# A Perceiver layer: both groups of a pair sorted in joint VectorE instructions, with a new ScalarE order

## What is computed

```python
k = k @ Wk.T                                    # 256 features, 16 heads of 16
x = abs(where(k >= 0, k, 0.01 * k)) + EPS
nrm = x.mean(-1)
k = softmax(log(x) * focusing_factor, -1) * nrm # "focus", over all 256 features
# in each head only the 11 largest of the 16 features are kept
kv = einsum('bnc,bnd->bcd', k_kept, v)          # sums over all rows of a batch
```

## Time and profile of the kernel before

| | us |
|---|---|
| median of 3 runs | 470.62 (470.41 to 471.29) |
| the profiled execution | 470.4 |
| its span, first to last instruction | 468.7 |
| around the span | 1.7 |
| VectorE busy | 447.6 (96%) |
| TensorE matmuls busy | 386.4 (82%) |
| ScalarE busy | 360.4 (77%) |

### The profile page before, as it was taken

How to read it: one execution, slowest core, us unless ns; L and a number is a source line. 1 busy time by engine, 2 the same in 40 slices (tenths; PEclk the granted TensorE clock), 3 DMA queues, 4 the chain that set the end, 5 groups by cost and what they waited for, 6 DMA issues and landing times.

```text
span 468.7 us, 6040 instructions
## 1 busy us (share of the span) xinstructions
PE 386.4 (82%) x1931; PEld 306.3 (65%) x1934; DVE 447.6 (96%) x685; ACT 360.4 (77%) x950; POOL 6.2 (1%) x22
## 2 busy tenths in 40 slices
PE   7986758989989998998997997991999899648567
PEld 6775547877877876886785885891987445314334
DVE  6999999999999999999999999999998889899995
ACT  2679997997997997997888978885438678666765
POOL 2001000000000000000000000000000000000000
PEclk9999879999999999999999999997799999956968
DMA  6990000320220220230140040022020000000001
GB/s 224 348 324 2 1 1 1 97 82 2 90 90 2 91 90 1 68 113 1 46 134 1 28 132 22 2 92 88 1 90 1 0 1 1 0 0 1 22 23 46
DMA packets 27071, 27.66 MB, mean 59 GB/s; under 512 B 1184, under 2 KB 26784, under 8 KB 27040
## 3 DMA queue, kind: packets, MB, share of 16 engines
q1 hardware_dynamic: 26736, 27.27, 18.2%
q0 software_dynamic: 160, 0.01, 0.0%
q10 hardware_dynamic: 144, 0.00, 0.0%
HBM read 26.22 MB, written 1.05 MB: 58 GB/s over the span
## 4 chain that ended last, share of the span: by engine, by line
DVE 86%; PE 6%; ACT 4%; issue 2%; DMA 1%; SPq 0%; DVEq 0%
DVE mask L1405 8%; DVE focus_words L1325 8%; DVE focus_words L1305 8%; DVE sorted L1361 4%; DVE merge L1374 4%; DVE sorted L1362 4%; DVE level L1331 4%; DVE level L1332 4%; DVE sorted L1234 3%; DVE amax L1203 2%; DVE sorted L1367 2%; DVE sorted L1366 2%; DVE keymax L1364 2%; DVE merge L1372 2%; DVE rank L1385 2%
## 5 line engine op out<-in xcount | busy, mean ns | idle before, releaser
L817 PE MATMUL bank<-WkT,rows_T 128*128 128x256 f32 x512 | 123.8, 388 | 29.4 <-ACT rows_T L434 29.4
L817 PEld LDWEIGHTS bank<-WkT,rows_T 128*128 128x128 f32 x512 | 94.3, 192 | 46.2 <-ACT rows_T L434 35.2
L909 PE MATMUL bank<-ctx_words,focus_words 128*128 128x257 f32 x512 | 115.3, 383 | 2.8 <-ACT focus_words L533 2.8
L909 PEld LDWEIGHTS bank<-ctx_words,focus_words 128*128 128x128 f32 x512 | 99.5, 197 | 15.1 <-ACT focus_words L533 4.4
L521 ACT ACTIVATE focus_words<-focus_words,shift,ff 128x256 f32<-128x256 f32 x136 | 79.8, 590 | 0.6
L487 ACT ACTIVATE focus_words<-bank 128x256 f32<-128x256 f32 x136 | 50.1, 382 | 25.7 <-PE bank L817 25.7
L533 ACT ACTIVATE focus_words<-focus_words,row_scale 128x256 f32<-128x256 f32 x136 | 56.2, 515 | 11.3 <-DVE row_scale L1318 11.3
L434 ACT ACTIVATE rows_T<-bank 128x512 f32<-128x512 f32 x78 | 44.3, 595 | 17.1 <-PE bank L790 16.9
L790 PE MATMUL bank<-ident,ctx_words 128*128 128x128 f32 x256 | 37.5, 275 | 3.8 <-DMA ctx_words<-in_ctx_dram 3.5
L1405 DVE TENSOR_TENSOR mask<-focus_words,fifth 128x2048 bf16<-128x2048 f32 x17 | 39.0, 2292 | 0.5
L790 PEld LDWEIGHTS bank<-ident,ctx_words 128*128 128x128 f32 x256 | 31.0, 142 | 11.7 <-DMA ctx_words<-in_ctx_dram 6.2
(11 more groups left out here) (207 smaller groups left out, 589.3 us busy)
## 6 DMA issues: line engine op xcount, KB each, us to landing
ctx_words<-in_ctx_dram SPq DMA_DIRECT2D x32, 512.0 KB, 3.9
ctx_words<-in_L_ffn_gate_w_dram SPq DMA_DIRECT2D x2, 1024.0 KB, 6.7
ctx_words<-in_L_ffn_up_w_dram SPq DMA_DIRECT2D x2, 1024.0 KB, 8.2
xs<-in_x_dram SPq DMA_DIRECT2D x4, 256.0 KB, 5.0
ctx_words<-in_L_ffn_down_w_dram SPq DMA_DIRECT2D x2, 512.0 KB, 10.7
ctx_words<-in_L_ffn_down_w_dram SPq DMA_DIRECT2D x1, 1024.0 KB, 4.8
out_dram<-xs SPq DMA_DIRECT2D x3, 256.0 KB, 2.1
gateT<-in_L_attn_W_qkv_dram SPq DMA_DIRECT2D x1, 512.0 KB, 7.0
```

The costliest lines, as they stand in the source:

```text
L817: ins = pe.matmul(proj_bank[m][:, t * D:(t + 1) * D], rows_T[:, m % 2, 2 * t + k, :], WT[:, k, :], start=(k == 0), stop=(k == KT - 1))
L909: ins = pe.matmul(sum_bank[k][:, 0:GW], heads_half(expo[slot][:, t, :], k), ctx_ring[:, s, t, :], start=(s == 0 and t == 0), stop=(s == PE ...
```

## The change

For the rounds a = 3 to 13:

- **DVE.** `level1`, `sorted4`, `rowmax` and the like get 16 tiles instead of 8, and the keys of both groups lie side by side. `sort_fours_of_both` replaces two `compare_pairs` and two `sort_fours`: 12 instructions over sixteen tiles (one comparison is cut in two) instead of 20 over eight. The row maxima of both groups come out together. `make_keys(d)` moves to the end of the round (in round 1 too; the last round has one `make_keys` less). `apply_mask(a)` comes directly behind `make_mask(a)`, with a `settle()` between, and `inverse_sums` behind it, with a `settle()` ahead of `row_scales`. `rank` and `low8` now lie in the memory of `level1`, which adds a `settle()` in the last round.
- **ACT.** The two small instructions on the row maxima run once for both groups. The order of the round is new (below); `logarithms` of the coming a moves to the end of the round before, and `scale_rows(a)` moves behind all four lifts of d and the weight quads.
- Buffers swap places (`key[0]` and `expo[0]`, and with them two buffers of the later part); PE's and SP's programs are as before.

The core of the diff:

```diff
@@ ACT pair(a, last)
-                logarithms(a, at(a))
+                if a == 1:
+                    logarithms(a, at(a))
...
+                else:
+                    rows_to_sbuf(c, 0)
+                    rows_to_sbuf(c, 1)
+                    logarithms(b, at(b))
+                    exponentials(a, at(a), FORE_TILES)
+                    rows_to_sbuf(c, 2)
+                    exponentials(a, at(a), HIND_TILES)
+                    rows_to_sbuf(c, 3)
+                    lift(c, 0, at(c))
+                    rows_to_sbuf(d, 0)
+                    lift(c, 1, at(c))
+                    rows_to_sbuf(d, 1)
+                    exponentials(b, at(b), FORE_TILES)
+                    lift(c, 2, at(c))
+                    rows_to_sbuf(d, 2)
+                    lift(c, 3, at(c))
+                    exponentials(b, at(b), HIND_TILES)
+                    rows_to_sbuf(d, 3)
+                    if at(a) == 0:
+                        save_sums((a - 1) // PER_BATCH)
+                    for m in range(PAIRS):
+                        lift(d, m, at(d))
+                if not last:
                     if d in REST_BEHIND:
                         q = QK_QUADS + 2 * REST_BEHIND.index(d)
                         weight_quad(q)
                         weight_quad(q + 1)
-                    lift(d, 2, at(d))
-                    lift(d, 3, at(d))
+                    scale_rows(a, at(a))
+                    logarithms(c, at(c))
                 scale_rows(b, at(b))
@@ DVE sort_fours_of_both(a), new
+                settle()
+                dve.wait_ge(keyed, a + 2)
+                step(tt(level1[:, :, 1:4:2, :], keys_of_both[:, :, 0:4:2, :], keys_of_both[:, :, 1:4:2, :], ALU.max))
+                for at in (of_pair(a), of_pair(a + 1)):
+                    step(tt(level1[:, at, 0:4:2, :], keys_of_both[:, at, 0:4:2, :], keys_of_both[:, at, 1:4:2, :],
+                            ALU.min))
+                    if at.start == 0:
+                        settle(but=1)
+                        step(tt(sorted4[:, :, 3, :], level1[:, :, 1, :], level1[:, :, 3, :], ALU.max))
                 settle(but=1)
                 step(dve.tensor_reduce(keymax[:, :], sorted4[:, :, 3, :], AX.X, ALU.max))
                 settle(but=1)
+                step(tt(sorted4[:, :, 2, :], level1[:, :, 0, :], level1[:, :, 2, :], ALU.max))
                 settle(but=1)
+                row_maxima(both, 2)
+                step(tt(sorted4[:, :, 0:5:4, :], level1[:, :, 0:2, :], level1[:, :, 2:4, :], ALU.min))
+                settle()
+                inner_twos(both)
+                join_fours(both)
@@ DVE pair(a, last), rounds 3 to 13
+                    sort_fours_of_both(a)
                     find_fifths(slice(0, 2 * T))
                 make_mask(a)
...
+                        dve.wait_ge(expo_ready, a + 1)
+                        settle()
+                        apply_mask(a, at(a))
+                        inverse_sums(b, BOTH_SLOTS)
                     settle()
                     row_scales(b, BOTH_SLOTS)
                 make_mask(b)
...
                     make_keys(c, at(c))
                     settle()
                     apply_mask(b, at(b))
+                    make_keys(d, at(d))
```

More of the change, by code:

```diff
@@ L508, in exponentials @@
                 slot = (s + 1) % 2
+                first = of_pair(n).start
                 if tiles[0] == 0:
[L511 to L514, removed]
+                    if searched_alone(n) or n % 2:
+                        of, count = (of_pair(n), 1) if searched_alone(n) else (slice(0, 2 * T), 2)
+                        act.wait_ge(rowmax_ready, n + count)
+                        act.activation(lnmax[:, of], rowmax[:, of], ACT.Ln, bias=EPS).then_inc(lnmax_done, count)
+                        act.wait_ge(lnmax_done, n + count)
+                        act.activation(shift[:, of], lnmax[:, of], ACT.Identity, scale=ff_neg[:, 0:1])\
+                            .then_inc(shift_done, count)
                     act.wait_ge(shift_done, n + 1)
@@ L553, in pair @@
                     tail_rows_to_sbuf("sums1", (proj_in_psum, PAIRS * (CGROUPS + 1)))
[L554 to L561, removed]
+                    exponentials(a, at(a), ALL_TILES)
+                    logarithms(b, at(b))
+                    if at(a) == 0:
+                        save_sums((a - 1) // PER_BATCH)
                     tail_rows_to_sbuf("sums2", (kv_in_psum, 1))
@@ L564, in pair @@
                     exponentials(b, at(b), ALL_TILES)
-                else:
+                elif a == 1:
+                    rows_to_sbuf(c, 0)
+                    rows_to_sbuf(c, 1)
+                    exponentials(a, at(a), ALL_TILES)
+                    logarithms(b, at(b))
+                    save_sums(0)
                     exponentials(b, at(b), FORE_TILES)
@@ L1348, in half_keys_and_pairs, with join_fours @@
                 step(tt(level1[:, tiles, 1:4:2, :], k4[:, :, 0:4:2, :], k4[:, :, 1:4:2, :], ALU.max))
-            def of_pair(n):
-                return slice(0, T) if n % 2 or n == 0 else slice(T, 2 * T)
             low, high = merge[:, :, 0:4, :], merge[:, :, 4:6, :]
             first_of, second_of = slice(0, HEADS), slice(HEADS, 2 * HEADS)
+            def join_fours(at):
+                settle(but=1)
+                step(tt(high[:, at], sorted4[:, at, 0:2, 0:32], sorted4[:, at, 0:2, 32:64], ALU.max))
+                settle(but=1)
+                step(tt(low[:, at], sorted4[:, at, 0:4, 0:32], sorted4[:, at, 0:4, 32:64], ALU.min))
@@ L1357, in sort_fours, with inner_twos, row_maxima @@
+            def inner_twos(at):
+                step(tt(sorted4[:, at, 1, :], sorted4[:, at, 4, :], sorted4[:, at, 2, :], ALU.min))
+                step(tt(sorted4[:, at, 2, :], sorted4[:, at, 4, :], sorted4[:, at, 2, :], ALU.max))
+            def row_maxima(at, groups):
+                dve.tensor_scalar(rowmax[:, at].bitcast(I32), keymax[:, at].bitcast(I32), -HD, key_flip[:, 0:1],
+                                  ALU.bitwise_and, ALU.bitwise_xor).then_inc(rowmax_ready, groups)
             def sort_fours(n):
-                slot, at = n % 2, of_pair(n)
+                at = of_pair(n)
@@ L1469, in pair @@
                 else:
-                    inverse_sums(b, BOTH_SLOTS)
-                    settle(but=1)
-                    apply_mask(a, at(a))
+                    if a == 1:
+                        inverse_sums(b, BOTH_SLOTS)
+                        settle(but=1)
+                        apply_mask(a, at(a))
+                    else:
+                        dve.wait_ge(expo_ready, a + 1)
+                        settle()
+                        apply_mask(a, at(a))
+                        inverse_sums(b, BOTH_SLOTS)
                     settle()
```

93 lines of the change are left out of this document (56 added, 37 removed).

## The result

| | us |
|---|---|
| before, median of 4 runs | 470.96 (470.41 to 471.98) |
| after, median of 4 runs | 500.62 (499.54 to 502.5) |
| ratio | 1.063 (95%: 1.0608 to 1.0651) |
| the profiled execution of after | 502.5, its span 500.7 |

What follows compares the result with a forecast made beforehand. The PE, ACT and load loop, 38.1 us against DVE's 36.3, was taken to bound the changed kernel: 470.4 plus 16.7 for the loop plus 12.6 for six clock falls gives 499.7, say 500; range 484 to 504.

Steps and rivals of the forecast that it cites:

- The six falls: TensorE's clock falls ahead of each sum of groups 1 to 11, at 2.1 us each, 12.6 together.
- DVE's list: DVE's instructions in rounds 3 to 13: 0.5 us saved a round, 36.3 instead of 36.8.
- The 0.11 for a new hole: Each new settle on DVE, as at apply_mask(a) behind make_mask(a), costs 0.11 us; two cost 0.22 a round.
- The loop: From one sum_group(a) to the next through load, PE and ACT: 38.1 us, plus save_sums and weight quads in some rounds.
- Both links: sum_group(a)'s start to quad 2 of c ready, 17.9 us; then ACT to scale_rows(a)'s end, 18.9 plus 1.3 of waits.
- the terms 18.9, 1.3, 0.6 and 1.1: From quad 2 of c to scale_rows(a)'s end: ACT's work 18.9 us, waits for PE 1.3, save_sums 0.6, weight quads 1.1.
- its wait for PE ahead of quad 2 of c: ACT, in rounds 3 to 13, would wait some 4 us for PE to have quad 2 of c ready.
- DVE's waits for the exponentials: DVE idle 2 to 5 us a round ahead of inverse_sums, until ACT's exponentials of b are done.
- The clock: PE idle 4.2 to 5.0 us ahead of sum_group(a) lowers TensorE's clock; each fall costs 1.7 to 2.5 us.
- The rival with the clock up: The loop is the bound but PE's gaps cause no fall: 487 us; no or few falls, 484 to 495, chance 0.25.
- the start of the loop: sum_group(1), behind the last lift and scale_rows(1), starts at 83.1 instead of 79.75.
- the loop has slack: Rival: DVE still sets the pace of the rounds, 467.5 us, faster; 466 to 469 has chance 0.09.

Runs made afterwards that it cites:

- the kernel with the exponentials first: Changed kernel with scale_rows(a) behind the first lift of d, all exponentials of a and half of b's ahead of quad 2 of c: 475.67 us.
- the kernel with half the filling: Changed kernel with 14 extra identity matmuls, results unread, on PE ahead of sum_group(a) in rounds 1 to 13: 490.42 us.
- the first filling: Changed kernel with 28 extra identity matmuls, results unread, on PE ahead of sum_group(a) in rounds 1 to 13: 497.6 us.

## Why the prediction was right

The forecast was 500; the median is 500.62, and it came by the steps that were named. That the two agree to 0.6 us is in part luck: the working gives 499.7 for the profiled execution, which took 502.5. The six falls, too, come to the forecast 12.6 in after (12.57), but to 10.36 and 11.93 in the two other profiled kernels with the same ACT order and no filling (the old sort and the further DVE instruction).

- **DVE's list**, forecast at 36.3 a round and 16.0 for the new sort: 36.36 in the kernel with the exponentials first, and 15.95 for the sort. So 0.41 of the 0.5 a round came. The 0.11 for a new hole is in the rows of round 3: from `make_mask(a)` at 106.78 to `apply_mask(a)` at 109.17 the step is 2.39, against 2.21 for the same instruction in the earlier trace rows; 0.18, a little more than the 0.11; the five later rounds have 2.39 to 2.40. The Trainium skill ("VectorE: DVE Perf Modes", The DRAIN you can't avoid), by which a semaphore between chained operations adds nothing, doesn't agree with this step.
- **The loop**, forecast at 38.1 and, with the weight quads and `save_sums`, at 39.2, 39.8, 39.2, 38.7, 38.1 and 38.7 for the six: 39.33, 39.89, 39.37, 38.79, 38.18 and 38.72 in after when the excess of the sums is taken off, 39.29, 39.93, 39.28, 38.78, 38.23 and 38.78 where the gap was filled. Both links hold. PE had quad 2 of c ready for ACT (147.70) 20.25 us after `sum_group(3)` had started, 17.98 without its fall, forecast 17.9. From that quad to the end of `scale_rows(5)` ACT took 21.9; the terms 18.9, 1.3, 0.6 and 1.1 make 21.9. ACT in round 5, with its wait for PE ahead of quad 2 of c, forecast at some 4 us:

```profile
147.70 0.60 ACT L444 ACTIVATE rows_T<-bank 128x512 f32<-128x512 f32 x1 [3.69 <-PE bank L830]
...
166.16 3.40 ACT L547 ACTIVATE focus_words<-focus_words,row_scale 128x256 f32<-128x256 f32 x8
```

  DVE's waits for the exponentials, forecast at 2 to 5 us a round, were 8.30, 5.18, 5.10, 4.54, 3.92 and 3.83: the first was well above.

- **The clock**, forecast at six falls of 1.7 to 2.5 and 12.6 together: 12.57, singly 1.64 to 2.87, behind gaps of 4.11 to 4.84 (forecast 4.2 to 5.0). The rival with the clock up, at 487, is the kernel with half the filling: its profiled execution took 487.82, its median 490.42.
- **What was mis-sized** is the start of the loop. `sum_group(1)` was forecast at 83.1 and began at 85.25. Of these 2.15, 0.64 were lost ahead of the projection that stood at 63.85 in the earlier trace rows and stands at 64.49 here. The rest is the fall behind this gap, which lasted longer: of these two projections the second one took 1.89 in the kernel before:

```profile
64.49 3.78 PE L857 MATMUL bank<-WkT,rows_T 128*128 128x256 f32 x8 [5.18 <-ACT rows_T L444]
...
68.92 2.75 PE L857 MATMUL bank<-WkT,rows_T 128*128 128x256 f32 x8
```

  With the 0.6 by which the loops were too short it makes the 2.7 between the forecast start of `sum_group(13)` (316.8 and 12.6, so 329.4) and 332.10, and so the 2.8 between 499.7 and the profiled 502.5. Five profiled kernels with the same round 1 up to its last projection, and with no filling that delays the sum (after, the half filling, the two with `scale_rows` earlier, and the further DVE instruction) began this sum at 85.25, 83.13, 85.33, 84.55 and 84.82. The median of after lies 1.9 below its profiled execution; that this start differs between executions would fit, but only one execution of each kernel has a trace.
- **The rivals.** That the loop has slack needed it under 36.3; it took 38.2 to 39.9. That it is ACT's order that decides, and that DVE's gain is real and buys nothing behind it, is shown by three kernels: the order alone with the old sort (504.0), the new sort with the order mended (475.7), and added DVE work at no cost (501.1).

## What to carry to other kernels

An engine that is busy for 77% of the span can set the pace when it closes a loop with another: follow one buffer around through the rounds, add up what lies between its free and its next free on each engine, and compare that sum with the list of the busiest engine before anything is put into an engine's order. Of what is moved, count what is now passed on the loop (here eight tiles of exponentials more and two lifts, 6.1 us), not whether the engine has idle time in all. Where such a loop opens an idle gap on TensorE ahead of work that lies on the loop, price the clock beside the gap; filling a part of the gap with matmuls that nobody reads tells the two apart.

## What was not expected of the hardware

- **Short gaps.** In the kernel with `scale_rows(a)` behind the first lift of d, sums took 8.90 instead of 7.22 behind gaps of 1.92 to 2.46 us, while behind 1.05 and 1.59 they took 7.22; the gap that the forecast was built on was 4.11. It was not the shortest with a fall in the kernel before: behind 3.65 us ahead of 407.69 the granted clock was 1.00 for 0.6 us and then 0.52. In the kernel with the exponentials first, gaps of 1.67 and 1.68 had no fall, nor had 1.72 with the half filling. But in after, ahead of the rounds, a projection took 3.28 instead of 1.99 behind a gap of 1.60, at a granted clock of 0.58 (0.98 in the 3 us ahead of it):

```profile
53.03 3.28 PE L857 MATMUL bank<-WkT,rows_T 128*128 128x256 f32 x8 [1.60 <-ACT rows_T L444]
```

  So the length of the gap alone does not decide. What PE had done ahead of these gaps was not varied: the sum of 7, behind 1.05, came after eight transposes of weights that the sums of 9, 11 and 13 don't have. The Trainium skill ("TensorE: Matmul & The Clock Gate", HAM oscillation) describes the loss in each repetition of a loop. The six sums of after agree with that; in the kernel with `scale_rows(a)` behind the first lift only three of the six sums of groups 3 to 13 have it, behind gaps about half as long as the one that the forecast was built on.
- **Two records for a matmul.** A 128 by 128 matmul of the identity with itself is recorded twice and takes 0.22 us, while the transposes with the same identity are recorded once, at a step of 0.43 for four. The kernel's own matmuls show the same: `project` issues four for the eight in the earlier trace rows and `sum_group` sixteen for the 32, so the counts of matmuls here are counts of records, and the length of the first filling could have been read from them. Whether a record is one pass over the array, no run shows.
